# Two attentions in one kernel: large loads issued by ScalarE's queue, small ones by SyncE's

## What is computed

```python
def reference(...):
    xn = _layernorm(x)
    s = _L0_attn_ref(xn, ...)   # 16 heads of 8 channels, learned bias by relative position, all keys
    g = _silu(_L0_ffn_ref(xn, ...))   # 8 routed experts (top 2) and 2 shared ones
    x = x + s * g
    xn = _layernorm(x)
    s = _L1_attn_ref(xn, ...)   # 16 heads of 8 channels, causal
    g = _silu(_L1_ffn_ref(xn, ...))   # gated single-head attention, then a gated mixture of 8 experts
    return x + s * g

# both attentions, per batch b and head h
att = softmax(q @ k.T * scale (+ bias or causal mask), axis=-1)
out = att @ v
```

## Time and profile before

| | us |
|---|---|
| median of 3 runs | 1297.9 (1286.46 to 1297.97) |
| the profiled execution, its own time | 1297.81 |
| its span, first to last instruction | 1295.6 |
| PE busy | 1120.1 (86%) |
| DVE busy | 801.1 (62%) |
| ACT busy | 648.2 (50%) |
| POOL busy | 193.9 (15%) |

### The profile page before, as it was taken

One profiled execution on the slowest core, in us unless ns is written; L12 is line 12 of the kernel. 1 busy time (PEld: TensorE's weight loads), 2 busy tenths in 40 slices (PEclk: granted clock), 3 DMA queues, 4 the chain that ended last, 5 costly groups with the idle time before them and its releaser, 6 DMA issues.

```text
span 1295.6 us, 19507 instructions
## 1 busy us (share of the span) xinstructions
PE 1120.1 (86%) x7306; PEld 521.1 (40%) x7306; DVE 801.1 (62%) x1582; ACT 648.2 (50%) x1246; POOL 193.9 (15%) x312
## 2 busy tenths in 40 slices
PE   5499999899799999997984885899999899897777
PEld 3366666222222222222142432444443367643444
DVE  6633333788699889884056854788882236465554
ACT  4323232158578778777434143656776322334344
POOL 2145563001011101001000001112221000001000
PEclk9699999679899999999586566889997599999888
DMA  4511224133101100100007231110123120000331
GB/s 130 192 74 61 90 89 88 50 76 76 43 19 35 44 27 27 35 14 15 10 9 220 75 77 37 51 52 19 55 89 120 48 67 1 0 1 1 131 131 33
DMA packets 62361, 78.06 MB, mean 60 GB/s; under 512 B 15856, under 2 KB 40128, under 8 KB 60224
## 3 DMA queue, kind: packets, MB, share of 16 engines
q1 hardware_dynamic: 62272, 76.87, 19.7%
HBM read 61.58 MB, written 14.62 MB: 59 GB/s over the span
## 4 chain that ended last, share of the span: by engine, by line
PE 61%; DVE 19%; ACT 6%; SPq 5%; DMA 5%; issue 2%; POOL 0%; DVEq 0%; ACTq 0%
PE PS L1511 60%; DVE mx L1304 11%; ACT arena L898 4%; SPq L543 3%; DMA sums<-arena 2%; DMA arena<-k_dram 1%; SPq L551 1%; SPq L562 1%; DMA arena<-drev_dram 1%; DVE arena L1485 1%; PE PS L1524 1%; DVE arena L1118 1%; DVE arena L1121 0%; DMA arena<-mrow 0%; DVE small L1471 0%
## 5 line engine op out<-in xcount | busy, mean ns | idle before, releaser
L1511 PE MATMUL PS<-arena 128*32 128x512 f32 (+13 forms) x3656 | 633.6, 505 | 78.8 <-DVE mx L1304 36.9
L898 ACT ACTIVATE arena<-PS 128x512 f32<-128x512 f32 (+3 forms) x896 | 437.5, 555 | 266.8 <-PE PS L1511 261.6
L1304 DVE TENSOR_REDUCE mx<-PS 128x1 f32<-128x512 f32 (+3 forms) x896 | 500.4, 623 | 98.1 <-PE PS L1511 97.2
L1511 PEld LDWEIGHTS PS<-arena 128*32 128x32 f32 (+3 forms) x3656 | 160.8, 107 | 463.3 <-DVE mx L1304 188.8
L1511 PE MATMUL PS<-x_hi,w_hi_lo 128*128 128x512 f32 x320 | 144.8, 494 | 1.0 <-DVE fw L1405 0.6
L1405 DVE TENSOR_TENSOR fw<-PS,fw 128x512 f32<-128x512 f32 x80 | 55.3, 691 | 119.7 <-ACT fw L945 118.0
L945 ACT ACTIVATE fw<-PS 128x512 f32<-128x512 f32 x80 | 47.8, 597 | 123.5 <-PE PS L1511 123.4
L836 POOL TENSOR_TENSOR fw<-fw,arena 128x512 f32<-128x512 f32 x64 | 84.9, 1327 | 88.8 <-DVE fw L1405 88.8
L1511 PE MATMUL PS<-fw 128*128 128x512 f32 (+3 forms) x184 | 90.3, 578 | 0.0
L789 POOL TENSOR_TENSOR arena<-arena,fw 128x512 f32<-128x512 f32 x32 | 41.1, 1284 | 286.0 <-DMA fw<-sum_dram 286.0
L1511 PEld LDWEIGHTS PS<-x_hi,w_hi_lo 128*128 128x128 f32 x320 | 61.2, 191 | 31.1 <-issue 19.4
(11 more groups left out here) (288 smaller groups left out, 1075.8 us busy)
## 6 DMA issues: line engine op xcount, KB each, us to landing
arena<-comb_dram SPq DMA_DIRECT2D x16, 1024.0 KB, 5.1
fw<-sum_dram SPq DMA_DIRECT2D x32, 256.0 KB
arena<-comb_dram SPq DMA_DIRECT2D x16, 512.0 KB, 7.3
arena<-k_dram SPq DMA_DIRECT2D x16, 408.0 KB
q_dram<-arena SPq DMA_DIRECT2D x24, 256.0 KB, 3.7
k_dram<-arena SPq DMA_DIRECT2D x24, 256.0 KB, 3.8
arena<-q_dram SPq DMA_DIRECT2D x16, 384.0 KB
arena<-drev_dram SPq DMA_DIRECT2D x32, 192.0 KB, 4.2
```

The source lines that it names most:

```text
L898: s.activation(Pr[:, m % 8, 0:w], bank(4 + m % 3, 0, w), ACT.Exp).then_inc(A["e_done"], 1)
L1304: v.reduce_max(mx[:, H % 2, kh, n:n + 1], bank(U % RING, 0, w), axis=AX.X, negate=True).then_inc(A["ring_free"], 1)
L1511: return nc.tensor.matmul(out_, lhsT, rhs, start=start, stop=stop)
```

## The change

Both queues now issue. `load_stacks`, `load_bias`, `load_rw` and `proj_weights` get the issuing engine as an argument. What SP issued at the start of each attention stays with SP (stacks 0 and 2 and bias 0 of layer 0, stack 0 of layer 1), and so do the last gate rows and the weights behind attention 1. The other large loads move into ACT's stream: in front of the first half, or at the start of a half, ahead of its exponentials. `attention_feed` is left with maxima, sums and the 64 KB store of the gates (`comb_out`).

```diff
+        def load_stacks(eng, l, n):
...
+                    eng.dma_start(dst, src).then_inc(att[l][f"ld{n}"], 16)
+        def load_bias(eng, G):
...
+                eng.dma_start(Hst[row:row + 64, parity, j // 2, :, :], src).then_inc(h_ld[parity], 16)
...
-            def attention_feed(l, then):
+            def attention_feed(l):
                 for H in range(LAG[l]):
                     max_rows(l, H)
-                    if H == 0:
-                        then.get(-1, nothing)()
                 for H in range(HALVES):
                     if H >= 1:
                         sums_out(l, H - 1)
-                    if l == 0 and H % 2 == 1 and H // 2 + 2 < GROUPS:
-                        sp.wait_ge(A["st_ps"], HG * steps_before(l, H))
-                        load_bias(H // 2 + 2)
-                    if H >= 1:
                         sums_back(l, H - 1)
                     if H + LAG[l] < HALVES:
                         max_rows(l, H + LAG[l])
-                    then.get(H, nothing)()
+                    if l == 1 and H == 8:
+                        comb_out()
...
-            attention_feed(1, {
-                -1: lambda: load_stacks(1, 1), 0: later_batch,
-                2: lambda: proj_weights(0, "q_proj"), 3: lambda: proj_weights(1, "k_proj"),
...
-            def attention(l):
+            def attention(l, loads):
...
                 m = 0
+                if -1 in loads:
+                    loads[-1]()
                 for H in range(HALVES):
+                    if H in loads:
+                        loads[H]()
                     for i, (kt, off) in enumerate(t_steps(l, H)):
...
+            def second_stacks():
+                act.wait_ge(drev_stored, 16 * PARTS * BATCH * 2)
+                act.wait_ge(ones_stored, 16 * 2)
+                load_bias(act, 1)
+                load_stacks(act, 0, 1)
+
+            def next_bias(H):
+                act.wait_ge(att[0]["st_ps"], HG * steps_before(0, H))
+                load_bias(act, H // 2 + 2)
+
+            def last_stacks():
+                load_stacks(act, 0, 3)
+                next_bias(1)
+
+            attention(0, {-1: second_stacks, 1: last_stacks, 3: lambda: next_bias(3), 5: lambda: next_bias(5),
+                          7: lambda: next_bias(7), 9: lambda: next_bias(9), 11: lambda: next_bias(11)})
...
+            def first_batch():
+                act.wait_ge(qk_stored[1][0], 16 * 12)
+                load_stacks(act, 1, 1)
+
+            def later_batch():
+                act.wait_ge(z_ready, 12)
+                act.wait_ge(qk_stored[1][1], 16 * 12)
+                load_stacks(act, 1, 2)
+                load_stacks(act, 1, 3)
...
+            attention(1, {
+                -1: first_batch, 1: later_batch,
+                3: lambda: projections(0, "q_proj"), 4: lambda: projections(1, "k_proj"),
+                5: lambda: projections(2, "v_proj"), 6: lambda: projections(3, "o_proj"),
+                10: lambda: rw_behind(7, 0), 11: lambda: rw_behind(7, 1), 12: lambda: rw_behind(7, 4),
+                13: lambda: rw_behind(11, 2), 14: lambda: rw_behind(11, 3), 15: lambda: rw_behind(7, 5)})
```

More of the change, by code:

```diff
@@ L484, in ffn_experts, with load_rw, proj_weights @@
             expert(9, 0, 72, 1, 3)
+        def load_stacks(eng, l, n):
+            for hh in range(2):
+                for dr, rows, at_ in ((q_dram[l], ROWS, q_at), (k_dram[l], TROWS, k_at)):
+                    src = bass.AP(tensor=dr.tensor, offset=(2 * n * HG + hh) * rows * SEQ,
+                                  ap=[[SEQ, rows], [2 * rows * SEQ, 2 * PAIRS], [1, SEQ]])
+                    dst = bf(at_[2 * n], 8)[64 * hh:64 * hh + rows, :].rearrange("p (r t) -> p r t", r=2 * PAIRS)
+                    eng.dma_start(dst, src).then_inc(att[l][f"ld{n}"], 16)
+        def load_bias(eng, G):
+            parity = G % 2
+            for j in range(HG):
+                row = 64 * (j % 2)
+                src = bass.AP(tensor=drev_dram.tensor, offset=(G * HG + j) * 2 * PARTS * DREV,
+                              ap=[[1, 64], [DREV, 2 * PARTS], [1, 256]])
+                eng.dma_start(Hst[row:row + 64, parity, j // 2, :, :], src).then_inc(h_ld[parity], 16)
+        rw_rows = [comb_dram[n].rearrange("(e t) k -> e (t k)", e=EXP) for n in (1, 2)]
+        def load_rw(eng, n, *experts):
+            for e in experts:
+                eng.dma_start(rwb[e], rw_rows[n][e].partition_broadcast(P)).then_inc(rw_in[e], 16)
+        def proj_weights(eng, n, name):
+            eng.dma_start(fw[:, n * 1024:(n + 1) * 1024].rearrange("p (e c) -> p e c", e=EXP),
+                          a["L1_ffn_" + name].rearrange("e c h -> c e h")).then_inc(fw_in, 16)
         block = ctx.enter_context(nc.Block())
@@ L534, in store_qk @@
                         sp.dma_start(dst, ksp[:, n, b * SEQ:(b + 1) * SEQ]).then_inc(qk_stored[l][b], 16)
[L536 to L551, removed]
             def max_rows(l, H):
@@ L645, in _ @@
             next_expert(7, 1, False)
-            load_stacks(0, 0)
-            load_stacks(0, 2)
+            load_stacks(sp, 0, 0)
+            load_stacks(sp, 0, 2)
             sp.wait_ge(drev_stored, 16 * PARTS * BATCH * 2)
             sp.wait_ge(y_done, 8 * (FFN_SEQ - 1))
[L650 to L675, removed]
-            rows = [comb_dram[n].rearrange("(e t) k -> e (t k)", e=EXP) for n in (1, 2)]
-            def load_rw(n, *experts):
-                for e in experts:
-                    sp.dma_start(rwb[e], rows[n][e].partition_broadcast(P)).then_inc(rw_in[e], 16)
+            load_bias(sp, 0)
             def comb_out():
@@ L686, in comb_out @@
                 sp.dma_start(comb_dram[1], combT[:, :]).then_inc(comb_stored, 16)
[L687 to L699 removed]
+            attention_feed(0)
+            store_qk(1, 0)
+            sp.wait_ge(qk_stored[1][0], 16 * 12)
+            load_stacks(sp, 1, 0)
+            store_qk(1, 1)
+            attention_feed(1)
             sp.wait_ge(att[1]["st_ps"], HG * steps_before(1, HALVES))
[L701 removed]
+            sp.wait_ge(comb_stored, 32)
+            load_rw(sp, 0, 6, 7)
             sp.wait_ge(fw_in, 16 * 4)
             sp.wait_ge(att[1]["r_done"], HALVES)
[L704 to L705 removed]
+            proj_weights(sp, 4, "w1")
+            proj_weights(sp, 5, "w2")
             for b in range(BATCH):
@@ L957, in _ @@
                 s.activation(n1T[:, 512 * c:512 * (c + 1)], bank(4 + c), ACT.Silu).then_inc(y_ev, 1)
-            attention(0)
+            def second_stacks():
[11 more added lines that the diff above has]
+                          7: lambda: next_bias(7), 9: lambda: next_bias(9), 11: lambda: next_bias(11)})
             copies(4, lambda c: xtok[:, 4 * c:4 * c + 4, :].rearrange("p t c -> p (t c)"), 8)
@@ L976, in _, with projections, rw_behind @@
             root_squares(1)
-            attention(1)
+            def first_batch():
[6 more added lines that the diff above has]
+                load_stacks(act, 1, 3)
+            def projections(n, name):
+                if n == 0:
+                    act.wait_ge(att[0]["r_done"], HALVES)
+                proj_weights(act, n, name)
+            def rw_behind(H, e):
+                act.wait_ge(comb_stored, 32)
+                act.wait_ge(att[1]["st_ps"], HG * steps_before(1, H + 1))
+                load_rw(act, 0, e)
+            attention(1, {
[4 more added lines that the diff above has]
+                13: lambda: rw_behind(11, 2), 14: lambda: rw_behind(11, 3), 15: lambda: rw_behind(7, 5)})
             def projected(c):
```

13 lines of the change are left out of this document (removed).

## The result

| | before | after |
|---|---|---|
| median of the runs | 1297.93 us (6 runs) | 1314.12 us (6 runs) |
| lowest to highest | 1286.46 to 1304.03 | 1308.09 to 1316.47 |
| ratio after / before | | 1.0123, 95% interval 1.0084 to 1.0161 |
| the profiled execution, its span | 1297.8, 1295.6 | 1308.1, 1305.8 |

The change costs 16.2 us. The profiled execution of the changed kernel is the lowest of its six runs, so the two profiles lie only 10.3 us apart.

A forecast was written before the change was run, and what follows sets the result against it. PE was busy 86% of the span with 61% of the chain, transfers some 10%; the change could reach only the two late sums. Terms 4 + 15 + 3 − 7.5 + 3.5 + 1 − 2 + 1.5 = +18.5 on 1297.8 gave 1316 us, range 1282 to 1333.

The forecast's parts named there:

- A: Main forecast: ACT is held at its queue as SP was; 1316 us, own range 1308 to 1326, chance 48%.
- Term 1: Start of attention 0: bias 0 lands later because ACT's loads share the engines; +4 us, between 0 and 8.2.
- Terms 2 and 3: Half 1 of attention 0: ACT held by its issues, +15 us; PE's slow clock behind it, +3.
- Term 4: Attention 0: first sums come in time, no longer behind stack 3's loads, so half 2 loses its surplus; −7.5 us.
- term 5: Halves 3, 5, 7, 9, 11: five more bias tiles issued by ACT, 0.7 us each; +3.5 us.
- Term 6: Start of attention 1: stack 1, issued earlier by ACT, runs beside half 0's maxima; +1 us, −1 to +5.
- term 7: Half 1 of attention 1: ACT held 19.1 us, late sums and one cold phase go; −2 us.
- Term 8: Four projection weights and six gate rows issued by ACT, 0.42 us each, partly hidden; +1.5 us.
- B: Rival: ACT isn't held, its queue takes eight transfers at issue cost; 1286 us, chance 24%.
- C: Rival: ACT is held only briefly, some 7 us each time, as two queues drain faster; 1299 us, chance 13%.
- D: Rival: SP is held along with ACT because issue is one shared unit, late sums remain; 1329 us, chance 15%.

The follow-up runs named there:

- e1: Changed kernel with bias 2 issued before stack 3 in half 1 of attention 0; 1301.69 us, ratio 1.0031.
- e2: Changed kernel with one wait added: ACT issues bias 1 and stack 1 only when bias 0 has landed; 1306.38 us, ratio 1.0070.
- e4: Changed kernel with each 51-row k stack issued as 48 rows and 3 rows; 1269.53 us, ratio 0.9790.
- e9: Kernel before with ScalarE issuing the sums of each half, everything else staying with SyncE; 1293.28 us, ratio 0.9954.
- e10: e7 with ScalarE issuing the sums; 1266.56 us, ratio 0.9736.
- e3: Changed kernel with stack 3 of attention 1 issued two halves later, at half 3; 1301.86 us, ratio 1.0041.
- e5: Kernel before, all on SyncE's queue, with each k stack cut into 48 rows and 3 rows; 1267.34 us, ratio 0.9801.
- e6: Changed kernel with k stacks cut as in e4 and stack 3 of attention 1 two halves later; 1264.00 us, ratio 0.9768.
- e7: e5 with stack 3 of attention 1 issued two halves later, all on SyncE; 1261.60 us, ratio 0.9756.
- e11: The kernel of e6 timed again, beside its twin on SyncE's queue alone; 1263.10 us, ratio 0.9764.
- e12: The kernel of e7 timed again, all on SyncE; 1268.13 us, ratio 0.9780.

## Why the prediction came right, term by term

The forecast was 1316.0, the median 1314.12; A happened, in the range and with the sign that held most of the chance. The mechanism, ScalarE held in both attentions and the sums freed, is what the traces show. That the number came within 2 us is in part luck: single terms missed by up to 4 us in both directions, as the table shows, and the misses cancel. "First sums of attention 0" in the prediction are those of half 1, the second ones (315.80); half 0's had left at 294.15. The terms, each read as the growth of the distance between the two traces:

| term | predicted | measured | how it is read |
|---|---|---|---|
| before the change acts | 0 | +1.9 | ACT's last evacuation in the expert network, 235.13 for 233.21 |
| 1 bias 0 shares the engines | +4 | +7.8 | landed 253.64 for 243.96 (235.75 + 8.21), less 1.9 |
| 2 and 3 hold, slow clock | +18 | +15.6 | sums of half 1 issued 341.06 for 315.80, less the 9.7 |
| 4 first sums in time | −7.5 | −7.6 | half 2 took 23.04 for 30.63 |
| 5 five bias tiles | +3.5 | 0.0 | the distance stays 17.67 |
| 6 start of attention 1 | +1 | +3.5 | mrow 5.29 us for 1.8 |
| 7 second hold for late sums | −2 | −4.3 | distance 17.0 behind it, from 21.3 |
| 8 weights, gate rows | +1.5 | about 0 | below |

The sum of the measured terms is +17; the medians say +16.2. (The distance of 17.0 is that of the second issue of sums in attention 1, 817.36 for 800.41; 21.3 is that at ACT's entry into half 1.) Behind 817 us the distance shrinks to 10. It loses 2.6 by the issue of sums at 884.15, over which PE's granted clock was 0.95 for 0.88 in the trace before, and 3.5 in the last half of attention 1, where the two traces read (columns as in the earlier trace rows):

```profile
1000.00:1025.00 25.00, 22.24 (x121) 5.72 (x113) 1.53 (x3) 11.91 (x29) 2.53 (x2) 0.50 0.06 20
```

```profile
1014.00:1036.00 22.00, 18.93 (x121) 4.75 (x113) 1.50 (x3) 12.20 (x29) 1.27 (x1) 0.68 0.05 15
```

The same work took 25.3 us before, at a granted clock of 0.50, and 21.8 after, at 0.68. The change has no part in it: from one issue of sums to the next, this half took 25.3 us also in e1, e2, e4, e9 and e10, and 16.6 us in e3, e5, e6, e7 and e11, at clocks of 0.98 to 1.00. Between e7 and e12, the same kernel in two profiled executions, it differs by 5.2 us. So a part of what separates two profiles, and of the spread of each kernel's runs, is the clock of this one stretch, and e1's profile shows how far that goes: its span, 1308.1, lies above that of the changed kernel, though its median is 12 us lower.

**Term 1 was undersized by half.** I took +4 between 0 and 8.2 from "sharing every engine half and half", and nearly the upper bound came. SyncE's own issue of the biases got longer too (16.07 for 14.82 us), and ACT's first stack issues behind it took 2.60, 1.66 and 5.35 us; ACT was idle and lost nothing. e2 takes the whole term out of the landing, and gets back 7 of the 7.8 us by the ratios, and 7.6 in the traces; its 5.2 us for the maxima is a price within that.

**Terms 2 and 3 were right in kind and 2.4 too high.** The series of the earlier trace rows gave 14.82 for the four biases; they took 15.62. PE, however, still did 3 us of work in the 16. e1 removes the hold, and its first sums leave at 304.30 for 317.63, 13.3 us earlier. But they now leave into the drain of the stacks: the next two intervals between issues of sums are 25.2 and 24.4 us where the changed kernel has 23.4 and 23.0, which leaves 10 us at that point and 12 by the ratios.

**Term 4 was exact, term 5 too dear.** The bias tiles cost 0.58 and 2.00 us of issue at 357.74, and ACT's idle time before its next exponential was 1.67 us; the half was no longer for it. My 0.7 us each assumed gaps of 2 us and no reserve; PE's three banks were that reserve.

**Term 6 and term 7 missed in opposite directions.** I had put stack 1 beside the maxima at +1 within −1 to +5; a 3 KB transfer beside a stack takes 5.2 to 5.3 us, in attention 1 here and in attention 0 in e2. In term 7 the hold was 20.0 us for my 19.1. The clock behind it was 0.50 for 4 us and 0.57 for 4 more, then full, so the cold phase that I had expected to vanish did.

**Term 8.** A projection weight costs ACT 0.37 to 0.45 us of issue, and ACT's idle row behind it reads 0.20 to 0.28, no more than usual. The distance doesn't grow over these halves; as it shrinks there with the clock, a price of 1 us or so could be hidden in it.

**A's own range** of 1308 to 1326 doesn't follow from the bounds named for it: those of terms 1, 2 and 5 add up to 1297 to 1332.

**The rivals.** B (ACT isn't held) falls with the two timelines above. C (held for 7 us) also: 17 and 20. D (SyncE held along with ACT) falls with SyncE's issues beside the holds. Its issues of maxima between 764.6 and 775.1, the last of them 0.7 us into ACT's hold, read

```profile
L572 SPq DMA_DIRECT2D arena<-mrow x7: 698/698/699, 764.6 to 775.1; - x7
```

(least, median and longest ns), and no issue of sums took over 0.63 us. The reverse is seen at 235: ACT issued four biases in 0.63 to 0.68 us each while SyncE stood in its 16.07. One issue in ACT's hold and four in SyncE's are few, but all are at plain cost. The exclusive lock that the Trainium skill describes ("Perfetto Trace Analysis", on the HWDGE DMA instruction) therefore doesn't cover the time of a hold. It isn't only its own queue that slows an issuer, though: the stack transfers behind these four biases took up to 5.35 us beside SyncE's, and 0.31 to 0.63 in e2 without them. How much of D lies in that isn't told apart here; in this kernel it cost nothing, as ACT was idle there. The other rule that I had weighed, "Issuing engines are not separate DMA queues", is right about the engines (term 1, the 5.3 us of term 6, the 15.58 us of e4) and not about standing in line: term 4 came in full.

What the prediction missed was the larger thing. It read the 8 us drains at a share of 0.25 as "few of the 16 engines carry them" and took them as given. Cutting them took 43 us off the changed kernel, where the change had cost 16. The change separates what suffers in the queue from what clogs it, and hands the clog to the one engine that PE can't do without.

## What to carry to other kernels

Before transfers are divided between queues, look at why the queue is slow: a DMA share of 0.2 while one transfer drains says that its shape uses few engines, and cutting 51 rows into 48 and 3 was worth 26 us on the kernel before (e5), where the division cost 16. An issuer that feeds the critical engine must never be the one whose fifth large transfer waits: count what stands ahead in its queue, put small and quick transfers first, and space the large ones. Moving a wait out of a queue helps only as far as the next small transfer of the same chain, so follow the chain to its end. And a wait in the chain is worth only the time until the next work is ready: of the 17.95 us ahead of attention 1, e5 won 0.9.

## What the runs showed of the hardware

- With little else in flight, four stack transfers were taken at issue cost by either issuer, and the next one held it until a k stack had drained: 7.33 and 7.29 us on ScalarE, 7.46 and 6.66 on SyncE. While one issuer was held, the other issued at plain cost (ScalarE's four biases 0.63 to 0.68 us, one of SyncE's maxima 0.70); but with both issuers' stacks in flight (share 1.04) ScalarE's stack transfers took 1.51 to 5.35 us to issue, against 0.31 to 0.63 without SyncE's (e2). With cut stacks twelve transfers, the bytes of eight uncut ones, passed in 5.7 us, none over 1.32 (e5), so it isn't a fixed number of transfers. In what unit the queue is full wasn't measured.
- Small transfers beside large ones pay on another queue as well. A 3 KB transfer took 5.2 to 5.3 us beside one stack, for 1.8 (and 1.77 in e4, where the cut stack was through by then); 8 KB of sums took 15.58 us beside two cut stacks.
- A cut transfer fills the engines (0.92 for 16 us in e4), so small transfers are slowed beside it too while it lasts; what it gains is that it ends earlier, two stacks within some 20 us for 35.
- The same half of attention 1 took 25.3, 21.8 or 16.6 us at granted clocks of 0.50, 0.68 and 0.98 to 1.00, in different executions, whatever the arrangement of the transfers.
